# Maximum pass written out, row factors and head projection made inside it, input in quarters, elu in halves

## The reference

```
L0  hW = h @ W[i];  hp = (adj > 0) @ hW;  hm = (adj < 0) @ hW        (3 heads, diagonal taken out)
    e+ = leaky([hp, hm] @ a);  e- = leaky([hm, hp] @ a)
    att = softmax(where(adj > 0, e+[j], where(adj < 0, e-[j], -9e15)));  support += (att * adj) @ hW
    two GRU cells: one on adj @ h, one on support / 3
L1  hyperbolic layer around adj @ tangent(x), weights 128 x 128
L2  GAT with one head: softmax over adj > 0 of leaky(src[j] + dst[i]);  x += elu(w @ h)
L3  spec = adj.T @ h;  x += adj @ (exp(-evals * t) * spec)
```

## Time and profile before

| what | value |
|---|---|
| median of 3 runs | 2898.05 us (2897.37 to 2902.49) |
| the profiled execution | 2897.09 us, span 2894.5 us |
| PE busy | 2193.6 us (76%) |
| DVE busy | 2028.7 us (70%) |
| ACT busy | 1482.7 us (51%) |
| bytes moved | 638.45 MB, mean 221 GB/s |
| granted TensorE clock, mean | 0.877 |

### The profile page before, as it was taken

How to read it: one execution, slowest core, us unless ns; L and a number is a source line. 1 busy time by engine, 2 the same in 40 slices (tenths; PEclk the granted TensorE clock), 3 DMA queues, 4 the chain that set the end, 5 groups by cost and what they waited for, 6 DMA issues and landing times.

```text
span 2894.5 us, 19594 instructions
## 1 busy us (share of the span) xinstructions
PE 2193.6 (76%) x5941; PEld 947.5 (33%) x5941; DVE 2028.7 (70%) x2441; ACT 1482.7 (51%) x1434; POOL 133.6 (5%) x220
## 2 busy tenths in 40 slices
PE   4674444444589999999987579950199995999997
PEld 3222111111234444444433334420033332444443
DVE  7986989989859888888956655589999995000000
ACT  1005888888867777777746713220288874000000
POOL 1001101010100000000000000002100000000000
PEclk9757777766699999999999889985599997999999
DMA  7999788888633333333330078967566663999994
GB/s 255 387 388 343 289 317 334 329 315 308 258 128 102 102 102 102 131 102 102 102 145 0 1 260 277 295 242 246 188 230 222 218 232 101 305 297 301 303 314 148
DMA packets 176907, 638.45 MB, mean 221 GB/s; under 512 B 11840, under 2 KB 16320, under 8 KB 133424
## 3 DMA queue, kind: packets, MB, share of 16 engines
q1 hardware_dynamic: 152192, 539.30, 53.9%
q0 software_dynamic: 24624, 98.03, 8.9%
HBM read 597.24 MB, written 40.04 MB: 220 GB/s over the span
## 4 chain that ended last, share of the span: by engine, by line
PE 58%; DVE 19%; issue 13%; ACT 4%; SPq 3%; DMA 2%; DVEq 1%; ACTq 0%; POOL 0%; POOLq 0%
PE bank L608 23%; PE bank L781 15%; DVE arena L1377 8%; PE bank L741 8%; PE bank L693 6%; SPq L269 3%; PE bank L746 2%; DVE arena L1356 1%; DVE arena L1240 1%; DVE arena L1165 1%; PE bank L596 1%; DVE arena L1593 1%; PE bank L628 1%; DMA arena<-in_adjT 0%; ACT arena L876 0%
## 5 line engine op out<-in xcount | busy, mean ns | idle before, releaser
L608 PE MATMUL bank<-arena 128*128 128x512 f32 x1536 | 661.6, 594 | 13.4 <-DVE arena L1462 13.4
L573 PE MATMUL bank<-arena 128*128 128x512 f32 x512 | 259.2, 668 | 295.1 <-ACT arena L883 234.6
L781 PE MATMUL bank<-arena 128*128 128x512 f32 x1024 | 444.3, 595 | 30.4 <-ACT arena L1117 30.4
L1377 DVE CUSTOM_DVE_ANT_0 arena<-arena 128x2048 f32<-128x2048 bf16 x192 | 436.6, 2323 | 28.0 <-ACT arena L876 16.9
L1462 DVE TENSOR_TENSOR arena<-arena 128x2048 f32<-128x2048 f32 x192 | 433.3, 2283 | 4.0 <-ACT arena L920 2.1
L876 ACT ACTIVATE arena<-arena,nmx 128x2048 f32<-128x2048 f32 x192 | 384.4, 2002 | 74.2 <-DVE nmx L1377 60.1
L608 PEld LDWEIGHTS bank<-arena 128*128 128x128 f32 x1536 | 292.6, 191 | 382.2 <-issue 382.0
L920 ACT ACTIVATE arena<-arena 128x2048 f32<-128x2048 f32 x128 | 244.5, 1911 | 142.8 <-DVE arena L1451 142.8
L1707 DVE TENSOR_TENSOR arena<-arena,bank 128x512 f32<-128x512 f32 x8 | 5.3, 686 | 417.2 <-PE bank L763 417.2
L781 PEld LDWEIGHTS bank<-arena 128*128 128x128 f32 x1024 | 194.5, 191 | 271.1 <-issue 240.3
L573 PEld LDWEIGHTS bank<-arena 128*128 128x128 f32 x512 | 107.8, 216 | 445.9 <-ACT arena L883 240.7
(11 more groups left out here) (235 smaller groups left out, 2100.0 us busy)
## 6 DMA issues: line engine op xcount, KB each, us to landing
arena<-in_adjT SPq DMA_DIRECT2D x384, 1024.0 KB, 5.2
arena<-in_adj SPq DMA_DIRECT2D x128, 1024.0 KB, 5.0
mask_d<-arena POOLq DMA_DIRECT2D x64, 512.0 KB, 7.0
arena<-mask_d POOLq DMA_DIRECT2D x64, 512.0 KB, 4.7
arena<-e_d POOLq DMA_DIRECT2D x6, 1024.0 KB, 11.5
arena<-nm_d POOLq DMA_DIRECT2D x6, 1024.0 KB, 6.9
arena<-gat_d POOLq DMA_DIRECT2D x6, 1024.0 KB, 5.2
arena<-in_x SPq DMA_DIRECT2D x4, 512.0 KB, 6.8
```

Of the source, the lines that this page charges most:

```text
L573: last = pe.matmul(banks[2][:], H[:, t, :], groups[4 + g % 4][:, b, :], start=(t == 0), stop=(t == T - 1))
L608: last = pe.matmul(banks[B * half + b][:], hW[:, t, h * C:(h + 1) * C], probs[k % 4][:, b * CH:(b + 1) * CH], start=(t == 0 and h == 0), s ...
L781: last = pe.matmul(banks[B * half + b][:], stationary[:, t, :], ring[slot][:, b * CH:(b + 1) * CH], start=(t == 0), stop=(t == T - 1))
L1377: v.tensor_tensor_reduce(logits[k % 3], mask, e_row, FAR_UNIT, FAR, ALU.add, ALU.min, nmx[:, k:k + 1]).then_inc(S["logits_ready"], 1)
```

## The change

- **Input.** The four small constants are loaded behind the first quarter of x. Statistics and factors are made for eight tiles at a time; the scaling with relu goes to ACT; values are copied and split by quarters; the first chunk of edge sums is woven into this on DVE (`edge_masks`) and PE (`edge_group`).
- **Maxima.** The loops are gone: 64 steps stand written out, in four parts in the order (rows 0, targets 0), (0, 1), (1, 1), (1, 0). Maxima and denominators go straight to their columns of `NM` and `DEN`. The first 2048 rows' factors are made at steps 33 to 45 and broadcast at step 48. In every second step POOL loads one tile of turned rows from memory (`hT_t`), PE projects it, ACT copies it to `hw_c`, and POOL stores it in `hw_d`.
- **Heads' pass.** The weights of each tile come from `hw_d` into a ring of five small slots, loaded by SP behind each tile; the second rows' factors are finished inside the pass. The GRU's operands are loaded during it.
- **Elu.** The first half of the rows is divided, put through elu and normalised inside the second half of the GAT pass (steps 44 to 59). The second half follows behind it. The spectral pass uses other banks and places (`H3`, `SPEC`, `spec_banks`), and waits for the rows group by group.

The core of the diff. Input and first edge sums, on DVE and then on PE:

```diff
+            def statistics_quarter(k):
+                cols = slice(k % 2 * G, k % 2 * G + G)
+                dve.wait_ge(x_loaded[k], 16)
...
+            statistics_quarter(0)
+            factors_quarter(0)
+            statistics_quarter(1)
+            dve.wait_ge(S["first_loaded"], 64)
+            v.memset(sums, 0.0).then_inc(S["sums_cleared"], 1)
+            edge_masks(0, 0)
+            factors_quarter(1)
+            edge_masks(0, 1)
+            for k in range(2):
+                split_quarter(k)
+                statistics_quarter(k + 2)
+                edge_masks(0, 2 * k + 2)
+                factors_quarter(k + 2)
+                edge_masks(0, 2 * k + 3)
...
+            for k in turn(0):
                 if k:
                     edge_values(k - 1)
+                if k >= 3:
+                    edge_group(0, k - 3)
```

The maxima on DVE, and the parts woven into them on POOL, PE and ACT:

```diff
-                with dve.Fori(0, 2) as i:
-                    for g in range(G):
...
-                            dve.wait_ge(S["logits_used"], i * (G * HEADS) + (2 * part * G * HEADS + k + 1))
-                            settle(dve, "dve_settled")
-                            v.tensor_tensor_reduce(logits[k % 3], mask, e_row, FAR_UNIT, FAR,
-                                                   ALU.add, ALU.min, nmx[:, k:k + 1]).then_inc(S["logits_ready"], 1)
...
-                    link(v.tensor_copy(col, nmx[:]))
+                for n in range(STEPS):
+                    part, j = n // PART, n % PART
+                    row, half = natural_order[part]
...
+                        dve.wait_ge(S["logits_used"], k + 1)
+                        v.tensor_tensor_reduce(logits[k % 3], mask, e_row, FAR_UNIT, FAR, ALU.add, ALU.min, NMF[:, col:col + 1])\
+                            .then_inc(S["logits_ready"], 1)
+                    dve.wait_ge(S["logits_ready"], HEADS * (n + 1))
+                    v.sem_inc(freed[n % 4], 1)
+                    if n == T + 1:
+                        final_maxima(0, link)
...
+                    if g % 2 == 0 and n:
+                        t = n // 2
+                        pool.wait_ge(S["hw_ready"], t)
+                        pool.dma_start(hT_t[:], hT_d[:, t * P:(t + 1) * P]).then_inc(S["hT_loaded"], 16)
+                    elif n > 1:
+                        store_weights(n // 2 - 1)
...
+                    if g % 2 == 0:
+                        t = (G * q + g) // 2
+                        pe.wait_ge(S["hT_loaded"], 16 * (t + 1))
+                        if t:
+                            pe.wait_ge(S["hw_copied"], t)
+                        pe.matmul(banks[1][:, 0:HEADS * C], hT_t[:], gw, start=True, stop=True).then_inc(S["hw_ready"], 1)
...
+                if n % 2 == 0 and n:
+                    copy_weights(n // 2 - 1)
```

The heads' pass on SP and DVE, the GAT pass on DVE, the spectral pass on PE:

```diff
+                        if n == HRING - 1:
+                            sp.wait_ge(S["logits_ready"], 2 * T * HEADS)
+                            sp.wait_ge(S["hw_stored"], 16 * T)
+                            for early in range(HRING):
+                                load_weights(early)
+                        elif n >= HRING:
+                            sp.wait_ge(S["probs_free"], HEADS * (n - HRING + 1) + 4)
+                            load_weights(n)
...
-                dve.wait_ge(heads_loaded[n % HRING], 16 * (n // HRING + 1))
+                dve.wait_ge(heads_loaded[n % HRING], 32 * (n // HRING + 1))
...
+                if n == T + 12:
+                    scale_half(0)
+                if T + 12 <= n < T + 16:
+                    elu_in(n - T - 12)
+                if T + 16 <= n < T + 20:
+                    elu_out(n - T - 16)
+                if n == T + 23:
+                    factors_half(0)
...
+                    if u == 2 and n == 0:
+                        pe.wait_ge(S["chunk_evacuated"], 2 * Q)
+                    if u == 2 and n == 1:
+                        turn_quarter(1, 2)
+                        turn_quarter(1, 3)
+                    if u == 2 and n == 2:
+                        turn_denominators(1)
```

More of the change, by code:

```diff
@@ L544, in _ @@
             for q in range(Q):
[L545 to L554 removed]
+                for g in range(G - 3 if q == 0 else 0, G):
+                    edge_group(q, g)
                     if g == 2 and q:
@@ L780, in stream @@
                     for b in range(B):
-                        last = pe.matmul(banks[B * half + b][:], stationary[:, t, :], ring[slot][:, b * CH:(b + 1) * CH],
+                        last = pe.matmul(banks[spec_banks[half][b]][:], stationary[:, t, :], ring[slot][:, b * CH:(b + 1) * CH],
                                          start=(t == 0), stop=(t == T - 1))
@@ new lines, in copy_support @@
+            def copy_support(q):
+                act.wait_ge(freed[G - 1], used[PASS_MAX] + 2 * q + 3)
+                if q:
+                    act.wait_ge(S["support_stored"], 16 * q)
+                act.activation(sup_c, banks[2][:], ACT.Copy).then_inc(S["support_copied"], 1)
+            for n in range(STEPS):
+                part, j = n // PART, n % PART
+                row, half = natural_order[part]
+                if n % 2 == 0:
+                    m = n + 1
+                    act.wait_ge(loaded[m % 4], 16 * (used[PASS_MAX] + m // 4 + 1))
+                    if row == half:
+                        act.wait_ge(S["blocks_cleared"], PART * half + j + 2)
+                    if n:
+                        act.wait_ge(S["odd_mask_stored"], 16 * (n // 2))
+                    act.activation(not_positive_edge, ring[m % 4], ACT.Relu, bias=ones[:], scale=-STEEP)\
+                        .then_inc(S["no_edge_ready"], 1)
+                for h in range(HEADS):
+                    k, col = HEADS * n + h, maximum_column(part, j, h)
+                    act.wait_ge(S["logits_ready"], k + 1)
+                    act.activation(logits[k % 3], logits[k % 3], ACT.Exp, bias=NMF[:, col:col + 1], scale=-1.0,
+                                   accum_out=DENF[:, col:col + 1]).then_inc(S["logits_used"], 1)
+                if n % G == 1 and n >= G:
+                    copy_support(n // G - 1)
+                if n % 2 == 0 and n:
+                    copy_weights(n // 2 - 1)
+                if n == T + 1:
+                    scale_factors(0)
+                if n == T + 4:
+                    log_denominators(0)
+                if n == T + 12:
+                    copy_row_factors(0)
@@ new lines, in split_quarter @@
+            def split_quarter(k):
+                dve.wait_ge(S["v_copied"], 2 * k + 2)
+                tiles = slice(G * k, G * k + G)
+                for part in range(3):
+                    src = V[:, tiles, :] if part == 0 else VR[:, tiles, :]
+                    dst = V19[:, tiles, 1 + 6 * part:7 + 6 * part]
+                    if part < 2:
+                        ch(v.tensor_copy(dst, src))
+                        tt(VR[:, tiles, :], src, dst, ALU.subtract)
+                    else:
+                        v.tensor_copy(dst, src).then_inc(S["v19_ready"], 2)
```

660 lines of the change are left out of this document (362 added, 298 removed).

## The result

The changed kernel takes 2810.91 us (median of 4 runs, 2807.62 to 2819.13) against 2900.03 for the kernel before on the same chip: a ratio of 0.970, 95% interval 0.967 to 0.972. Run once more beside other kernels it took 2814.58 us, ratio 0.970 (0.969 to 0.972). Forecast were 2815.5 us and a range of 2783 to 2852. The profiled execution has a span of 2806.3 us, 88.2 less than before.

A forecast was written before the change was run, and what follows sets the result against it. No engine bounds the whole: maxima are DVE's, heads' and spectral passes PE's, the first stage its loads'. Terms -5 - 15 - 32 - 9 - 21.5 = -82.5 take 2898 to 2815.5 us; range 2783 to 2852.

The forecast's parts named there:

- Step 1: First stage: input in quarters, first edge sums begun inside it, -5 us, bounds 0 and -17.5.
- Step 2: Stage of the maxima: loops written out and projections added, -15 us, bounds -35 and +31.
- DVE's side: Maxima: writing out removes most of DVE's idle time, -35 us after the added factor operations.
- The transfers' side: Maxima: a chunk of eight tiles takes 65.5 us with the added bytes, against 67.4 before, so the gain is -15.
- Step 3: Seam from last maximum to heads' pass: projections, turning and row factors' sums leave it, -32 us, bounds -36 and -24.
- the sign named for being right: First seam: 15 to 17 us from the last maximum to the first head's matmul.
- Step 4: Entry of the GRU: operands loaded during the heads' pass and PE starts warm, -9 us, bounds -5 and -11.
- Step 5: Elu in halves: -36 us in the seam to the spectral pass, +14.5 in the GAT pass, together -21.5.
- the transfers' case: Rival, 20%: transfers take the maxima's gain; the stage stays at 539 us or grows by 31, total 2831 to 2862.
- The others: Rivals: maxima keep all (17%, 2790 us), elu costs what it saves (5%, 2837), slower (5%, 2947), no effect (1%).
- POOL's chain of a mask store, turned rows and weights: Slower rival, 5%: in the maxima this chain, through POOL's single order, becomes the pair's clock at 20.5 us, total 2947.

The follow-up runs named there:

- the run with the whole input: The changed kernel with DVE waiting for all four quarters of x before its first statistics: 2819.77 us, ratio 0.972.
- the loops alone: The kernel before with only DVE's and ACT's loops of the maxima's stage written out, projections left in the seam: 2867.61 us, ratio 0.988.
- the run with early weights: The changed kernel with the first five tiles' weights loaded without waiting for the store of the 32nd projection: 2809.13 us, ratio 0.969.
- the run that has one: The changed kernel with the first half's elu and layernorm moved out of the GAT pass to behind it: 2813.83 us, ratio 0.970.
- the run with five projections: The changed kernel with 5 of the 32 projections in the maxima's stage, only its times being read: 2807.16 us, ratio 0.968.

## Why the prediction was right, step by step

**Step 1, -5: measured -3.6** (and -2.7 the second time). The mechanism stands: between 30 and 60 us the queue has shares of 0.67 and 0.44 for 15 us each, so 13.4 us of transfer are unused, where the same stretch before has 0.48 and 0.33, 17.9 us: 4.5 less. That the queue is gated by slots that come free late is shown by the run with the whole input, where the same order 8 us later ends 8 us later.

**Step 2, -15: measured -19.5 and -16.7.** Right in the kind of reason, and near in size. DVE's side was taken as -35: the loops alone gave 28.5, with 6.6 us of waits for tiles left, so that term was right. The own completions, which I put at 0.4 us a pair of tiles, stand as 0.59 in the changed kernel's idle time (7.8 + 6.0 + 3.1 + 1.9 over 32 pairs), and two of them cost 0.16 of lost overlap more. The transfers' side was taken as 65.5 us a chunk; it was 65.0, and the runs show that it takes two causes together: without the slow stretch at each eighth tile it is 63.7, and without most of the added bytes, but with the stretch, 64.3. The queue held 415 GB/s behind the gap, more than the 382 of the earlier trace rows, and so more than the sum had. The Trainium skill's 358 GB/s for one core, in "DMA: Bandwidth & Descriptors", section Bandwidth, was rightly not taken as a limit. The Trainium skill's "HBM Reference", section Specifications (TRN2), says that a core streaming alone gets about 425, and the trace agrees: 415 at a share of 1.03.

**Step 3, -32: measured -29.9.** The mis-sized term is the store of the last projection: 3.0 us were taken with its issue, and 764.71 to 771.22 is 6.5. The loads behind it took 2.4 instead of 3.5, which gave 1.1 back, and from DVE's first operation on it was 6.1 as said. With 17.8 us from the last maximum to the first head's matmul the sign named for being right, 15 to 17, was missed. The size of the store hardly counts there: the median landing of these stores of 192 KB is 6.0 us, and the 7.0 of the larger mask stores, named as the bound, was nearly it. DVE's jump, 5.77 us before, indeed lay beneath, as the run with early weights showed by uncovering it. The logarithm of the second rows cost 0: the heads' pass has 0 idle time of PE behind its first matmul.

**Step 4, -9: measured -8.1**, which is the wait of 7.29 and the last steps. The 2 us for a warm start are there at the entry and lost again behind it. PE's first three pairs of matmuls took 2.07, 1.91 and 1.49 us before and take 1.02 each in both executions of the changed kernel, but from the GRU's first matmul to the hyperbolic pass it is 177.7 us in the second execution against 178.0 before. That one has a granted clock of 0.74 over 1540 to 1580 and 0.66 over the last 42.4 us, where the kernel before had 0.86 and 0.70 in the stretches that answer to these.

**Step 5, -36 and +14.5: measured -35.7 and +13.8**, and -1.1 behind. Both terms came out, and the argument for the second holds, inserted work less a lead; the sum -21.5 is -21.9. Inside the second, errors cancel: the inserted work was 16.9 us for the 18.6 taken, lead and slack met 3.4 of it for the 5.9 taken, and ACT's table loads made DVE wait 0.46 us where ACT's part was put at 2. The cold start, taken as 3, cost 2.6 in the run that has one. What the prediction didn't ask is whether the inserted part earns its 13.8: it doesn't.

That the total came within 5 us is in part luck. Step 2 brought 2 to 4.5 us more than was said, and step 3 brought 2 less and step 1 one to two less. The GRU's stage gave 4.5 in the profiled execution that no step had and the second one took back.

Of the rivals, the transfers' case was a third right: 9 us of the maxima's 28.5. The others didn't happen; for POOL's chain of a mask store, turned rows and weights, the run with five projections leaves at most 5.6 us in the whole stage.

## What to carry to other kernels

A stage that streams evenly is not bound by its mean rate: look in slices of 10 us for the place where the consumer stands, here for one bank, and see what removing that gives before counting bytes. Work moved beneath another stage is free only up to the lead that its engine has there; price both the place it leaves and the place it enters, since here all of it was worth nothing, and half of it 7 to 10 us. An engine that waits for its own last result only to pass on a signal can pass it on one instruction later, at the price of a slot that comes free later.

## What was not expected of the hardware

A wait of DVE on its own result cost 0.29 us from the end of one maximum to the start of the next, plus the 0.08 us by which unwaited maxima overlap; with a clearing as the next operation, 0.23 in all. Taking both out of a pair of tiles, with the slot's return moved, took 20.3 us off the stage over 64 tiles.

In six of the eight chunks of the changed kernel one maximum takes 3.2 us instead of 2.29. The last, at 749.47:

```profile
748.50 2.06 POOL L441 TENSOR_TENSOR arena<-arena,not_i 128x512 f32<-128x512 f32 x1
749.47 3.24 DVE L1540 CUSTOM_DVE_ANT_0 arena<-arena 128x2048 f32<-128x2048 bf16 x1
```

In all six POOL is clearing a diagonal when the maximum starts. In a seventh chunk the maximum starts first, at 529.76, and POOL's clearing at 529.84; there the maximum takes 2.29 us and the clearing 3.23. So the one that starts second is the longer one. The kernel before has seven such maxima, of 3.24 to 3.29 us. The Trainium skill, in "Advanced Engine Details and Errata", section VectorE Performance Modes, says that DVE's second port is shared with GpSimd; no run here took POOL's operation away to show it.

A store of 192 KB in a busy stage lands in 6.0 us in the median, hardly sooner than one of 512 KB (7.3).

DVE's jump over the branch not taken cost 6.20 us of issue in the run with early weights, and merging the two conditions took the seam from 13.2 to 9.4 us. The Trainium skill, in "Advanced Engine Details and Errata", section Control Flow Timing, gives about 51 ns for a branch and 108 ns with a comparison. By that figure the merge would have been worth an estimated 0.1 us; what the rest of the 6.20 is, no run here tells.
